# Decoder layer in float32: the scores of the windowed self-attention as one multiplication of 96 stacked rows per head

## The chip, the cores and the metric

One core of a Trainium2 chip runs the whole program. The metric is the device time of one execution in microseconds, lower is better; of several runs the median is given. TensorE multiplies, ScalarE (ACT), VectorE (DVE) and GpSimd (POOL) do the elementwise work, and SyncE (SP) issues the DMA transfers.

## What is computed

A decoder layer on x of 2 x 1024 rows of 512 numbers, in float32: windowed self-attention, cross-attention to a context of 2 x 2048 rows, and a gated feed-forward part, each behind a layer norm and added to its input. The change touches the self-attention:

```python
qkv = x @ qkv_w.T + qkv_b
q, k, v = jnp.split(qkv, 3, axis=-1)              # 16 heads of 32
q = q / (jnp.linalg.norm(q, axis=-1, keepdims=True) + 1e-6)
k = k / (jnp.linalg.norm(k, axis=-1, keepdims=True) + 1e-6)
diff = j - i
allowed = (jnp.abs(diff) <= 16) & (jnp.mod(diff, 2) == 0)
scores = jnp.where(allowed, jnp.einsum('bhnd,bhmd->bhnm', q, k), -jnp.inf)
out = jnp.einsum('bhnm,bhmd->bhnd', jax.nn.softmax(scores, axis=-1), v)
x = x + out @ out_w.T + out_b
```

Only positions of one parity see each other, so the host lays the rows out as four sequences of 512 rows, in which a row sees the 8 before and the 8 behind it.

## The kernel before

**Precision.** TensorE's fast float32 type (float32r) keeps fewer bits, so each operand is split into a rounded high part, made by ScalarE, and the rest as a low part, made by VectorE or GpSimd. A product is the sum of high x high, high x low and low x high (`three`, L187), three multiplications into one PSUM bank.

**Units.** A sequence has 16 units (`UN`): 4 groups of 4 heads, times 4 tiles of 128 keys. For a unit, `scores` (L1151) multiplies the keys of a tile with the queries in a window of 136 or 144 columns; ScalarE takes `exp` of it; GpSimd multiplies with the band (`mask`, L505); `weighted` (L1169) adds the tile's weighted values and the sums of the weights, for each head, to two PSUM banks that a group keeps for its four units. `copy_out` (L643) copies both banks, VectorE takes the reciprocal of the sums in two halves (`inverse`, L903), GpSimd multiplies (`out_scale`, L512), ScalarE rounds (`out_hi`) and GpSimd makes the low part (`out_lo`, L519). `project_out` (L1187) then multiplies all four groups of a sequence with the output weights.

**Scores before.** `heads` (L1113) turns the keys and queries of a group (four heads of 32 rows, 128 in all) by transposes. `heads_hi` (L626) and `heads_lo` (L892) write the parts. The queries are written twice, each time masked (`hmask`) to every second head, side by side, so that one multiplication of 64 rows gives two heads in 272 or 288 columns. Three products times two row halves are six multiplications for a unit.

**Slots.** The order of all queues is written by hand: a sequence is 16 slots, and slot n of sequence s holds one unit and a piece of other work. On TensorE:

- slots 0 to 3: projection of the second half of queries and keys of s
- slots 4 to 7: its values, the output projection of sequence s - 1 (one tile of 128 rows a slot, from slot 4), transposes of the input of s + 1
- slots 8 to 11: queries and keys of s + 1 (first half), transposes of sequence s - 1's result for cross-attention
- slots 12 to 15: values of s + 1, cross-attention queries of s - 1; in the last sequence the first cross-attention scores

`heads(s, 2)` is in slot 6, `heads(s, 3)` in 7, `heads(s + 1, 0)` in 14, `heads(s + 1, 1)` in 15. Slot n opens with `scores(s, n + 1)` and closes with `weighted(s, n)`; slots 7 and 15 (`LATE`) have the scores at their end. The other engines follow the same slots: GpSimd's list for n = 1 has mask 2 and `out_scale` of the last group of the sequence before, n = 2 has mask 3, its `out_lo` and two of the four bias additions (`out_bias`), then a small norm operation (`root1`), n = 3 mask 4 and the two other bias additions. `inverse` of that group is in VectorE's n = 0 and 1. SP waits for x tiles, stores and reloads the residual tile `xs` (`store`, `store_q`, L429, L442), and in the last sequence loads the first context pieces (`load_ct`).

Ring banks of PSUM (`Ring`) are taken in a fixed order (`ring_uses`); the change leaves that order as it is.

Of the kernel before, what the change touches and what calls it, by code (L numbers as in the profile page):

```python
# [49 lines left out]
LATE = (7, 15)  # L50
# [174 lines left out]
def attention_phase(nc, ctx, plan, sem, score, ident, mhalf, wait_pad, q_const, work, ring, links,  # L225
# [14 lines left out]
    qbd_h = sb("qbd_h", [P, 2, 2, SEQ], F32R)  # L240
    qbd_l = sb("qbd_l", [P, 2, 2, SEQ], F32R)
    kt_h = sb("kt_h", [P, 2, SEQ], F32R)
    kt_l = sb("kt_l", [P, 2, SEQ], F32R)
# [8 lines left out]
    over_ot = Plan(nc, plan.at)  # L252
    ot_h = sb("ot_h", [P, HG, SEQ], F32R)
# [3 lines left out]
    over_x2t = Plan(nc, plan.at)  # L257
    x2t_h = sb("x2t_h", [P, DK, SEQ], F32R)
# [10 lines left out]
    hmask = sb("hmask", [P, 2])  # L269
# [42 lines left out]
    CONSTS = 8 + HPG  # L312
# [51 lines left out]
    kq_hi = sem("kq_hi")  # L364
    s_ready = sem("s_ready")
# [13 lines left out]
    def window(i):  # L379
        lo, hi = max(0, P * i - HALO), min(SEQ, P * i + P + HALO)  # L380
        return lo, hi - lo, lo - (P * i - HALO)

    x1_v = x1_dram.rearrange("(s t p) d -> s p t d", t=ST, p=P)

    with nc.Block() as block:
        @block.sync
        def _(sp):
# [35 lines left out]
            sp.dma_start(ob_row[:], out_b.partition_broadcast(P)).then_inc(ob_landed, 16)  # L423
            for s in range(NS):
                for k in range(ST * (s + 1) + 3, min(ST * (s + 2) + 3, ST * NS)):
                    next_tile(k)
                if not s:
                    sp.wait_ge(set_lo, WO + 1)
                    sp.dma_start(xs[:], x_v[0]).then_inc(xs_landed, 16)  # L429
                if s:  # L430
                    store(s - 1)
                if s == NS - 1:
# [3 lines left out]
                    for n in range(5):  # L436
                        cross.load_ct(sp, n)
                if s:
# [19 lines left out]
        def _(pool):  # L458
            PL = nc.gpsimd

            def constants(pool):
# [4 lines left out]
                PL.memset(hmask[:], 0.0).then_inc(consts, 1)  # L466
                pool.wait_ge(consts, 5)
                for h in range(HPG):
                    PL.memset(hmask[DH * h:DH * h + DH, h % 2:h % 2 + 1], 1.0).then_inc(consts, 1)
                pool.wait_ge(consts, 5 + HPG)  # L470
# [4 lines left out]
                pool.wait_ge(consts, 7 + HPG)  # L475
# [58 lines left out]
            mask(0, 0)  # L534
            for s in range(NS):
                more = s + 1 < NS
                for n in range(UN):
                    if n not in LATE:
                        mask(s, n + 1)
                    if n == 1 and s:  # L540
                        out_scale(group(s, -1))
                    if n == 2 and s:
# [12 lines left out]
                    if n in (6, 9, 13):  # L555
                        out_scale(group(s, n // 4 - 1))
                    if n == 7:
                        mask(s, 8)
                    if n in (7, 10, 14):
                        out_lo(group(s, {7: 0, 10: 1, 14: 2}[n]))  # L560
                    if n == 15 and more:
                        mask(s + 1, 0)
# [10 lines left out]
        def _(act):  # L573
# [118 lines left out]
            heads_hi(0, 1)  # L692
            product_hi(2)
            product_hi(3)
            exp(0, 0)
            for s in range(NS):
                more = s + 1 < NS
                for n in range(UN):
                    t = n % ST
                    if t == 0 and (s or n):  # L700
                        copy_out(group(s, n // 4 - 1))
                    if n not in LATE:
                        exp(s, n + 1)
# [4 lines left out]
                    if n < 4:  # L708
                        squares(s, 1, t)
                        if n == 2 and s:  # L710
# [6 lines left out]
                    elif n < 12:  # L717
                        for m in value_parts(s, n):
# [3 lines left out]
                        if n == 10:  # L722
                            if s:
                                norm2(s - 1, 3)
# [1937 lines left out]
```

## Time and profile before

| | us |
|---|---|
| median of 3 runs | 1193.99 (1193.2 to 1194.45) |
| profiled execution, its own time | 1193.53 |
| its span in the trace | 1191.5 |
| TensorE busy | 1151.1 (97%) |
| VectorE busy | 872.4 (73%) |
| ScalarE busy | 548.3 (46%) |
| GpSimd busy | 431.7 (36%) |
| mean granted TensorE clock | 0.991 of 2.4 GHz |

Busy TensorE means that a multiplication was in flight; matmuls overlap, so a busy share near one says that the queue hardly ever waits, not that the array is full. The self-attention stage runs from about 49 to 380 us of the span, the cross-attention from there to about 830, the feed-forward part to the end.

### The profile page before, as it was taken

The numbers are of one execution on the slowest core, as the hardware profiler recorded it, in microseconds if no ns is written. First come the engines' busy times: TensorE is split into PE (matmuls) and PEld (weight loads), VectorE is DVE, ScalarE is ACT, GpSimd is POOL, SyncE is SP. The second block draws the span as 40 slices with busy tenths as digits, with TensorE's granted clock in tenths as the row PEclk, the third lists the DMA queues.
The fourth block names the chain that finished last, engine by engine and source line by source line (L and its number), as shares of the span: only waits on it lengthen the run. The fifth ranks groups of instructions, "written<-read, shape, count | busy, mean of one in ns | idle before, by whom it ended". The sixth has DMA issues, their size and how long they took to land.

```text
span 1191.5 us, 17227 instructions
## 1 busy us (share of the span) xinstructions
PE 1151.1 (97%) x6432; PEld 935.4 (79%) x6432; DVE 872.4 (73%) x1352; ACT 548.3 (46%) x862; POOL 431.7 (36%) x383
## 2 busy tenths in 40 slices
PE   7999999999989999999999997999999998999998
PEld 6777778777767888888888885878778887888886
DVE  6666675684684657876687798875899878888775
ACT  5354454455364345554445444554444445444431
POOL 1255765665753300200020034022445842444431
PEclk9899999999989999999999998999999999999999
DMA  8001010200133434333334332223311111511101
GB/s 292 9 28 45 10 63 1 80 37 23 50 111 130 166 132 142 115 101 142 121 125 149 116 121 73 80 80 123 124 54 54 54 53 63 170 53 53 53 18 71
DMA packets 53570, 103.88 MB, mean 87 GB/s; under 512 B 4848, under 2 KB 17136, under 8 KB 52464
## 3 DMA queue, kind: packets, MB, share of 16 engines
q1 hardware_dynamic: 53488, 102.78, 25.8%
q8 instruction: 52, 0.85, 0.3%
q14 instruction: 30, 0.25, 0.1%
HBM read 85.99 MB, written 16.78 MB: 86 GB/s over the span
## 4 chain that ended last, share of the span: by engine, by line
PE 81%; DVE 9%; ACT 4%; issue 3%; POOL 3%; ACTq 0%; DVEq 0%; POOLq 0%
PE work L189 15%; PE work L190 14%; PE work L191 14%; PE score L189 4%; PE score L190 4%; PE score L191 4%; PE score L2523 4%; PE score L2524 4%; PE score L2525 4%; PE score L1165 2%; PE work L2523 2%; PE work L2525 2%; PE work L2524 2%; PE score L1179 1%; PE work L1092 1%
## 5 line engine op out<-in xcount | busy, mean ns | idle before, releaser
L508 POOL TENSOR_TENSOR probs<-probs,band 128x544 f32<-128x544 f32 (+1 forms) x64 | 92.4, 1444 | 87.3 <-ACT probs L639 87.0
L2196 POOL TENSOR_TENSOR hid<-fg,hid 128x512 fp32r<-128x512 f32 x48 | 84.4, 1778 | 106.5 <-ACT hid L2263 106.5
L189 PE MATMUL score<-pt_h,cn_h 128*128 128x512 f32 x256 | 101.8, 398 | 9.5 <-DVE pt_l L1672 5.9
L1512 POOL TENSOR_TENSOR xr<-xr,bv_row 128x512 f32<-128x512 f32 x16 | 27.3, 1731 | 228.1 <-DMA xr<-x_scratch 228.1
L190 PE MATMUL score<-pt_l,cn_h 128*128 128x512 f32 x256 | 100.6, 393 | 0.0
L191 PE MATMUL score<-pt_h,cn_l 128*128 128x512 f32 x256 | 100.5, 393 | 0.0
L189 PE MATMUL work<-x_q_h,ct_h 128*128 128x512 f32 x256 | 100.3, 392 | 0.0
L191 PE MATMUL work<-x_q_h,ct_l 128*128 128x512 f32 x256 | 99.7, 389 | 0.0
L190 PE MATMUL work<-x_q_l,ct_h 128*128 128x512 f32 x256 | 99.7, 389 | 0.0
L2402 DVE SCALAR_TENSOR_TENSOR fx<-work,fx 128x512 f32<-128x512 f32 x96 | 65.7, 685 | 40.2 <-PE work L191 40.2
L189 PE MATMUL work<-wqkv_h,xt_h 128*128 128x512 f32 (+1 forms) x256 | 94.0, 367 | 0.0
L2523 PE MATMUL score<-fxt,w_hl 128*128 128x512 f32 x236 | 92.3, 391 | 1.5 <-DVE fxt L2350 0.8
L2525 PE MATMUL score<-fxt,w_hl 128*128 128x512 f32 x236 | 91.9, 389 | 0.0
L2524 PE MATMUL score<-fxt,w_hl 128*128 128x512 f32 x236 | 91.8, 389 | 0.0
L2184 POOL TENSOR_TENSOR wsum<-w_stage 128x256 f32<-128x256 f32 x24 | 18.4, 765 | 194.0 <-ACT w_stage L2220 138.3
L190 PE MATMUL work<-wqkv_l,xt_h 128*128 128x512 f32 (+1 forms) x256 | 87.5, 342 | 0.0
L191 PE MATMUL work<-wqkv_h,xt_l 128*128 128x512 f32 (+1 forms) x256 | 87.4, 342 | 0.0
L1566 ACT ACTIVATE x_pr<-x_s 128x512 f32<-128x512 f32 x52 | 33.0, 634 | 94.4 <-DVE x_s L1668 94.4
L2263 ACT CAST hid<-fg 128x512 fp32r<-128x512 f32 x48 | 29.7, 621 | 87.5 <-DVE fg L2387 52.8
L189 PE MATMUL work<-wd_h,hid 128*128 128x512 f32 x176 | 68.7, 391 | 0.6 <-DVE fx L2402 0.6
L1672 DVE TENSOR_TENSOR pt_l<-x_pr,pt_h 128x512 fp32r<-128x512 f32 x64 | 51.3, 802 | 24.4 <-ACT pt_h L1570 23.6
L191 PE MATMUL work<-wd_h,hid 128*128 128x512 f32 x176 | 68.5, 389 | 0.0
(254 smaller groups left out, 3176.1 us busy)
## 6 DMA issues: line engine op xcount, KB each, us to landing
ct_raw<-in_ctx_t SPq DMA_DIRECT2D x32, 512.0 KB, 4.6
cn_raw<-in_ctx_n SPq DMA_DIRECT2D x32, 512.0 KB, 3.8
w_stage<-in_wg_t SPq DMA_DIRECT2D x12, 512.0 KB, 4.1
w_stage<-in_wu_t SPq DMA_DIRECT2D x12, 512.0 KB, 3.8
wd_raw<-in_wd_t SPq DMA_DIRECT2D x12, 512.0 KB, 3.7
x_in<-in_x SPq DMA_DIRECT2D x16, 256.0 KB, 2.8
xs<-in_x SPq DMA_DIRECT2D x4, 1024.0 KB, 5.2
x_scratch<-xs SPq DMA_DIRECT2D x4, 1024.0 KB, 4.7
```

Of the source, the lines that this page charges most:

```text
L189: pe.matmul(out, hi_s, hi_m, start=first, stop=False)
L190: pe.matmul(out, hi_s, lo_m, start=False, stop=False)
L191: return pe.matmul(out, lo_s, hi_m, start=False, stop=last)
L508: PL.tensor_tensor(probs[:, n % 2, :, 0:w], probs[:, n % 2, :, 0:w], band[:, c0:c0 + w].unsqueeze(1).to_broadcast([P, HPG, w]), ALU.mult). ...
L1566: A.activation(pr[:, j % 2, :], s_at(j), ACT.Exp).then_inc(e_done, 1)
L1672: V.tensor_tensor(pt_l[:, j % 2, :], pr[:, j % 2, :], pt_h[:, j % 2, :].bitcast(F32), ALU.subtract)\
L2196: PL.tensor_tensor(hid[:, q, 1, :], g[:, q, :], hid[:, q, 0, :].bitcast(F32), ALU.subtract).then_inc(hidl_done, 1)
L2263: A.copy(hid[:, q, 0, :], g[:, q, :]).then_inc(hidh_done, 1)
L2402: V.scalar_tensor_tensor(xs[:, t, :], work[:, 2 + n % 2, :], WSCALE, xs[:, t, :], ALU.mult, ALU.add)\
L2523: PE.matmul(bank(key), w_h, x_h, start=first, stop=False, skip_group_check=True)
L2524: PE.matmul(bank(key), w_h, x_l, start=False, stop=False, skip_group_check=True)
L2525: last = PE.matmul(bank(key), w_l, x_h, start=False, stop=k == 1, skip_group_check=True)
```

## The change

- The four heads' keys and queries are no longer masked. `heads_hi` and `heads_lo` write four tiles (keys high and low, queries high and low) into one of three places (`turned_heads`).
- SP then moves rows by transfers from SBUF to SBUF (`stack_heads`): for each head, 96 stacked rows, keys high, low, high over queries high, high, low. A group's transfers are two halves of columns, 12 transfers in each: 4 heads x 3 parts, each 32 rows with 264 or 248 columns of keys and of queries (about 64 KB). The first half may be overwritten once unit 2 of the group before is multiplied, the second after its unit 3.
- `scores` is one multiplication of 96 rows for each head, four a unit, each of 136 or 144 columns. TensorE waits for a half (`stacked`) before units 0 and 2 of a group.
- Slot n opens with `scores(s, n)` and closes with `weighted(s, n - 1)`, without exceptions for slots 7 and 15. `copy_out`, `inverse`, `out_scale`, `out_hi`, `out_lo` and the masks move accordingly. `project_out` and `out_bias` stay in their slots.

The diff, cut to its core:

```diff
+MOVED = 3 * 4 * 16
...
+            def stack_heads(s, g, b):
+                k = group(s, g)
+                if b == 0:
+                    wait_freed(sp, ("qt", s, g))
+                if k:
+                    sp.wait_ge(s_ready, ST * (k - 1) + 3 + b)
+                c = slice(SEQ // 2 + HALO, SEQ) if b else slice(0, SEQ // 2 + HALO)
+                parts_of, (k_h, k_l, q_h, q_l) = turned_heads(g)
+                for h in range(HPG):
+                    r = slice(DH * h, DH * h + DH)
+                    for i, (of_k, of_q) in enumerate(((k_h, q_h), (k_l, q_h), (k_h, q_l))):
+                        sp.dma_start(stack[DH * i:DH * i + DH, h, :, c].bitcast(F32),
+                                     parts_of[r, of_k:of_q + 1:of_q - of_k, c].bitcast(F32)).then_inc(stacked[b], 16)
...
+            for b in range(2):
+                stack_heads(0, 0, b)
             for s in range(NS):
-                for k in range(ST * (s + 1) + 3, min(ST * (s + 2) + 3, ST * NS)):
+                for b in range(2):
+                    stack_heads(s, 1, b)
+                tiles = range(ST * (s + 1) + 3, min(ST * (s + 2) + 3, ST * NS))
+                for k in tiles[:3]:
                     next_tile(k)
                 if not s:
                     sp.wait_ge(set_lo, WO + 1)
                     sp.dma_start(xs[:], x_v[0]).then_inc(xs_landed, 16)
+                stack_heads(s, 2, 0)
+                for k in tiles[3:]:
+                    next_tile(k)
+                stack_heads(s, 2, 1)
                 if s:
                     store(s - 1)
                 if s == NS - 1:
                     wait_freed(sp, ("qk", s, 1, ST - 1))
                     cross.load_q(sp, 0)
                     wait_filled(sp, ("qt", s, 3))
-                    for n in range(5):
+                    for n in range(2):
                         cross.load_ct(sp, n)
+                stack_heads(s, 3, 0)
+                if s == NS - 1:
+                    cross.load_ct(sp, 2)
+                stack_heads(s, 3, 1)
+                if s == NS - 1:
+                    for n in range(3, 5):
+                        cross.load_ct(sp, n)
+                if s + 1 < NS:
+                    for b in range(2):
+                        stack_heads(s + 1, 0, b)
                 if s:
                     store_q(s - 1)
...
 (GpSimd)
-            mask(0, 0)
             for s in range(NS):
                 more = s + 1 < NS
                 for n in range(UN):
-                    if n not in LATE:
-                        mask(s, n + 1)
-                    if n == 1 and s:
+                    mask(s, n)
+                    if n == 2 and s:
                         out_scale(group(s, -1))
-                    if n == 2 and s:
+                    if n == 3 and s:
                         out_lo(group(s, -1))
                     if n in (2, 3) and s:
                         out_bias(s - 1, 2 * n - 4)
...
-                    if n in (6, 9, 13):
-                        out_scale(group(s, n // 4 - 1))
...
                     if n in (7, 10, 14):
-                        out_lo(group(s, {7: 0, 10: 1, 14: 2}[n]))
+                        out_scale(group(s, {7: 0, 10: 1, 14: 2}[n]))
+                    if n in (8, 11, 15):
+                        out_lo(group(s, {8: 0, 11: 1, 15: 2}[n]))
...
 (ScalarE)
             def heads_hi(s, g):
+                parts_of, (k_h, _, q_h, _) = turned_heads(g)
+                k = group(s, g)
+                if k >= 2:
+                    for b in range(2):
+                        act.wait_ge(stacked[b], MOVED * (k - 1))
                 wait_filled(act, ("kt", s, g))
-                A.copy(kt_h[:, g % 2, :], bank(("kt", s, g))).then_inc(kq_hi, 1)
+                A.copy(parts_of[:, k_h, :], bank(("kt", s, g))).then_inc(kq_hi, 1)
                 wait_filled(act, ("qt", s, g))
-                for j in range(2):
-                    A.mul(qbd_h[:, g % 2, j, :], bank(("qt", s, g)), hmask[:, j:j + 1]).then_inc(kq_hi, 1)
+                A.copy(parts_of[:, q_h, :], bank(("qt", s, g))).then_inc(kq_hi, 1)
...
-                    if t == 0 and (s or n):
+                    if t == 1 and (s or n > 1):
                         copy_out(group(s, n // 4 - 1))
-                    if n not in LATE:
-                        exp(s, n + 1)
+                    exp(s, n)
...
-                        if n == 2 and s:
+                        if n == 3 and s:
                             out_hi(group(s, -1))
...
 (VectorE)
-                for j in range(2):
-                    last = V.scalar_tensor_tensor(qbd_l[:, g % 2, j, :], bank(("qt", s, g)), hmask[:, j:j + 1],
-                                                  qbd_h[:, g % 2, j, :].bitcast(F32), ALU.mult, ALU.subtract)
-                last.then_inc(dve_freed, 1)
+                V.tensor_tensor(parts_of[:, q_l, :], bank(("qt", s, g)), parts_of[:, q_h, :].bitcast(F32),
+                                ALU.subtract).then_inc(dve_freed, 1)
...
-                    if n in (0, 1) and s:
-                        inverse(group(s, -1), n)
+                    if n in (1, 2) and s:
+                        inverse(group(s, -1), n - 1)
...
 (TensorE)
-                if i == 0:
-                    wait_freed(pe, ("qt", s, g))
+                if i % 2 == 0:
+                    pe.wait_ge(stacked[i // 2], MOVED * (group(s, g) + 1))
                 if u:
                     pe.wait_ge(exp_done, u)
-                out = [scb[:, a, 0:2 * WIN].rearrange("p (h w) -> p h w", h=2)[:, :, 0:w] for a in range(2)]
-                c = slice(P * i, P * i + P)
-                for kt, qt, first_mm, last_mm in ((kt_h, qbd_h, True, False), (kt_h, qbd_l, False, False),
-                                                  (kt_l, qbd_h, False, True)):
-                    for a in range(2):
-                        r = slice(64 * a, 64 * a + 64)
-                        last = PE.matmul(out[a], kt[r, g % 2, c], qt[r, g % 2, :, lo:lo + w],
-                                         start=first_mm, stop=last_mm)
+                for h in range(HPG):
+                    out = scb[:, h // 2, WIN * (h % 2):WIN * (h % 2) + w]
+                    last = PE.matmul(out, stack[0:3 * DH, h, 0, P * i:P * i + P], stack[0:3 * DH, h, 1, lo:lo + w],
+                                     start=True, stop=True)
...
-                    if n not in LATE:
-                        scores(s, n + 1)
+                    scores(s, n)
...
                     if n == 7:
-                        scores(s, 8)
                         heads(s, 3)
                     if n == 15 and more:
-                        scores(s + 1, 0)
                         heads(s + 1, 1)
-                    weighted(s, n)
+                    if n:
+                        weighted(s, n - 1)
+                    elif s:
+                        weighted(s - 1, UN - 1)
```

## Rows read from the trace of the kernel before

**Rows 1.** Busy time of a stretch, the third sequence: us, then each engine's busy time (count), clock, DMA

```profile
211.50:297.00 85.50, 85.00 (x708) 66.84 (x704) 56.84 (x126) 42.06 (x77) 52.30 (x49) 1.00 0.12 41
```

**Rows 2.** Timeline, TensorE, third sequence: start us, duration us, engine, line, what

```profile
219.78 0.39 PE L1165 MATMUL score<-qbd_h,kt_h 64*128 64x272 f32 x2
...
228.04 0.40 PE L1165 MATMUL score<-qbd_h,kt_h 64*128 64x288 f32 x2
...
230.18 0.40 PE L189 MATMUL work<-wo_h,ot_h 128*128 128x512 f32 x1
```

**Rows 3.** Timeline, TensorE, around one unit's weighted sums and scores

```profile
304.15 0.39 PE L190 MATMUL work<-wqkv_l,xt_h 128*128 128x512 f32 x1
304.38 0.39 PE L191 MATMUL work<-wqkv_h,xt_l 128*128 128x512 f32 x1
...
305.89 0.50 PE L189 MATMUL work<-wqkv_h,xt_h 128*128 128x512 f32 x1
306.23 0.40 PE L190 MATMUL work<-wqkv_l,xt_h 128*128 128x512 f32 x1
```

**Rows 4.** Timeline, TensorE, around weighted sums with no scores behind them

```profile
326.66 0.39 PE L191 MATMUL work<-wo_h,ot_l 128*128 128x512 f32 x1
...
327.60 0.39 PE L189 MATMUL work<-wqkv_h,xt_h 128*128 128x256 f32 x1
327.83 0.28 PE L190 MATMUL work<-wqkv_l,xt_h 128*128 128x256 f32 x1
...
328.06 0.28 PE L189 MATMUL work<-wqkv_h,xt_h 128*128 128x256 f32 x1
```

**Rows 5.** Groups of TensorE's weight loads, third sequence: busy us, mean ns

```profile
L190 PEld LDWEIGHTS work<-wqkv_l,xt_h 128*128 128x128 f32 x64 | 12.1, 189 | 1.0
```

**Rows 6.** Waits, TensorE, whole span: us in total, times, longest

```profile
PE score L1179 <- ACT o_sc L648: 1.7, 4, 0.5
```

**Rows 7.** Timeline, GpSimd, slots 2 to 4 of the third sequence

```profile
222.71 1.29 POOL L517 TENSOR_TENSOR o_sc<-o_sc,rsum 128x512 f32<-128x512 f32 x1 [4.18 <-DVE rsum L906]
223.95 1.37 POOL L508 TENSOR_TENSOR probs<-probs,band 128x544 f32<-128x544 f32 x1
225.37 1.29 POOL L522 TENSOR_TENSOR ot_l<-o_sc,ot_h 128x512 fp32r<-128x512 f32 x1
226.62 2.53 POOL L527 TENSOR_TENSOR xs<-xs,ob_row 128x512 f32<-128x512 f32 x2
229.11 0.55 POOL L483 TENSOR_TENSOR rstd<-ve,mhalf 128x1 f32<-128x1 f32 x1
...
229.98 1.36 POOL L508 TENSOR_TENSOR probs<-probs,band 128x544 f32<-128x544 f32 x1
```

**Rows 8.** Timeline, SP's issues: start, us for all of them, how many

```profile
0.79 1.33 SPq L403 DMA_DIRECT2D x_in<-in_x  x3
...
490.50 2.08 SPq L1459 DMA_DIRECT2D xr<-x_scratch  x4
```

**Rows 9.** Transfers: size of each, median us from issue to landing

```profile
x_in<-in_x SPq DMA_DIRECT2D x16, 256.0 KB, 2.8
...
out_y<-fx SPq DMA_DIRECT2D x16, 256.0 KB, 2.0
```

**Rows 10.** Timeline, VectorE's and TensorE's, first sequence: groups turned late, units behind them

```profile
87.36 0.69 DVE L895 TENSOR_TENSOR kt_l<-work,kt_h 128x512 fp32r<-128x512 f32 x1 [0.98 <-ACT kt_h L628]
...
93.83 0.40 PE L1165 MATMUL score<-qbd_h,kt_h 64*128 64x288 f32 x2
...
119.84 0.69 DVE L895 TENSOR_TENSOR kt_l<-work,kt_h 128x512 fp32r<-128x512 f32 x1
...
125.94 0.40 PE L1165 MATMUL score<-qbd_h,kt_h 64*128 64x288 f32 x2
```

**Rows 11.** Busy time of two stretches, last sequence, columns as in rows 1

```profile
344.00:350.00 6.00, 2.96 (x44) 1.72 (x36) 4.07 (x8) 4.35 (x7) 5.02 (x4) 0.95 0.00 0
350.00:356.00 6.00, 5.23 (x12) 4.11 (x13) 5.93 (x8) 2.81 (x5) 2.92 (x2) 0.50 0.00 1
```

More of the change, by code:

```diff
@@ L239, in attention_phase @@
     over = Plan(nc, plan.at)
[L240 to L243, printed above, removed]
+    stack = sb("stack", [P, HPG, 2, SEQ], F32R)
+    heads_even = sb("heads_even", [P, 4, SEQ], F32R)
     probs = sb("probs", [P, 2, HPG, WIN])
@@ L252, in attention_phase @@
     over_ot = Plan(nc, plan.at)
+    heads_ot = Plan(nc, plan.at).put("heads_ot", [P, 2 * HG, SEQ], F32R)
     ot_h = sb("ot_h", [P, HG, SEQ], F32R)
@@ L257, in attention_phase @@
     over_x2t = Plan(nc, plan.at)
+    heads_x2t = Plan(nc, plan.at).put("heads_x2t", [P, 2 * DK, SEQ], F32R)
     x2t_h = sb("x2t_h", [P, DK, SEQ], F32R)
@@ L364, in attention_phase @@
     kq_hi = sem("kq_hi")
+    stacked = [sem(f"stacked{b}") for b in range(2)]
     s_ready = sem("s_ready")
@@ L381, in window, with turned_heads @@
         return lo, hi - lo, lo - (P * i - HALO)
+    def turned_heads(g):
+        return {1: (heads_x2t, (2, 3, 4, 5)), 3: (heads_ot, (2, 3, 6, 7))}.get(g, (heads_even, (0, 1, 2, 3)))
     x1_v = x1_dram.rearrange("(s t p) d -> s p t d", t=ST, p=P)
@@ L465, in constants @@
                 PL.memset(ones[:], 1.0).then_inc(consts, 1)
[L466 to L470, printed above, removed]
+                pool.wait_ge(consts, 4)
                 PL.affine_select(out=ident[:], in_=ident[:], compare_op=ALU.not_equal, fill=1.0,
@@ L717, in _ @@
                     elif n < 12:
+                        if n == 8:
+                            out_hi(group(s, 0))
                         for m in value_parts(s, n):
@@ L721, in _ @@
                             squares(s + 1, 0, t)
-                        if n == 10:
-                            if s:
-                                norm2(s - 1, 3)
+                        if n == 10 and s:
+                            norm2(s - 1, 3)
+                        if n == 11:
                             out_hi(group(s, 1))
@@ L751, in _ @@
                     if n == 7:
-                        exp(s, 8)
                         heads_hi(s, 3)
-                        if s:
-                            wait_filled(act, ("o", s - 1, ST - 1))
-                        out_hi(group(s, 0))
                     if n == 15 and more:
-                        exp(s + 1, 0)
                         heads_hi(s + 1, 1)
@@ L1000, in _ @@
                         spread1(s + 1, {1: 0, 2: 1, 3: 2, 5: 3}[n])
-                    if n in (0, 1) and s:
-                        inverse(group(s, -1), n)
-                    if n in (5, 6):
-                        inverse(group(s, 0), n - 5)
-                    if n in (8, 9):
-                        inverse(group(s, 1), n - 8)
-                    if n in (12, 13):
-                        inverse(group(s, 2), n - 12)
+                    if n in (1, 2) and s:
+                        inverse(group(s, -1), n - 1)
+                    if n in (6, 7):
+                        inverse(group(s, 0), n - 6)
+                    if n in (9, 10):
+                        inverse(group(s, 1), n - 9)
+                    if n in (13, 14):
+                        inverse(group(s, 2), n - 13)
                     if n < 4:
@@ L1223, in _ @@
             heads(0, 0)
-            heads(0, 1)
             product(2)
             product(3)
-            pe.wait_ge(prod_lo, 2)
-            scores(0, 0)
+            heads(0, 1)
             bias_columns()
@@ L1271, in _ @@
                     if n == 7:
[L1272 removed]
                         heads(s, 3)
                     if n == 15 and more:
[L1275 removed]
                         heads(s + 1, 1)
[L1277 removed]
+                    if n:
+                        weighted(s, n - 1)
+                    elif s:
+                        weighted(s - 1, UN - 1)
             s = NS - 1
+            weighted(s, UN - 1)
             for j in (4, 5, 6):
```

22 lines of the change are left out of this document (8 added, 14 removed).

## The prediction

> **What bounds the kernel now.** I read the busy times of a stretch first, then the unit starts, then TensorE's timeline of one unit, then the queues that it waits for. In the third of the four sequences of the self-attention stage TensorE is busy for 85.0 of 85.5 us, at full granted clock [rows 1], and none of the other engines for more than two thirds. So what leaves TensorE's queue there is a gain, and what makes it wait is a loss, unless another wait goes with it. The order of its work is written by hand in slots. In the kernel before, slot n opens with the scores of unit n+1, so the score row at 219.78 opens slot 2 of that sequence, and the one at 228.04 opens slot 4: two slots of projection take 8.26 us [rows 2].
>
> **The multiplications.** Now six multiplications make a unit's scores, in three pairs of 64 rows. From the last steady matmul ahead of the weighted sums (304.38) to the second projection matmul after the scores (306.23) it is 1.85 us; two matmuls of 512 columns belong to that, 0.23 each (304.15 to 304.38), so sums and scores cost 1.39 [rows 3]. Where the sums stand alone, from 326.66 to 327.83 it is 1.17; less 0.23 for the 512-column matmul and 0.12 for the 256-column one (327.83 to 328.06 holds two) that is 0.82, with both changes of array shape in it [rows 4]. The scores therefore cost 0.57 us a unit. After the change four multiplications of 96 rows and at most 144 columns use the same shape as the projection that follows, so they need no change of shape of their own. Each needs a load of 128 columns of weights. What such a pair costs is not in this trace for 96 rows. The shortest full-height stream is the 256-column one at 0.12 [rows 4]. By columns alone it would be 144/256 of that, 0.065. Without any overlap of load and multiplication it is the 0.23 of the first matmul after a change of shape (327.60 to 327.83) [rows 4]. I take 0.12, because one load is seen for 189 ns [rows 5] and a load of the same rows cannot be put beside the last one as the 64-row pairs are; the ends stay for the range. Four cost 0.48: 0.09 saved, times 64 units is **-6 us**. At 0.065 it would be -20, at 0.23 +22.
>
> The Trainium skill ("TensorE: Matmul & The Clock Gate", Back-to-back issue gap) gives about 81 ns for a sustained pair of load and 128-column multiplication; estimated from that page, a unit would cost 0.33 us and the whole saving would be 15 us instead of 6. The same page (LDWEIGHTS) puts a load at columns over 1.2 GHz, 107 ns for 128, which agrees with my 0.12 better; no run here shows which holds for 96 rows.
>
> **ScalarE, VectorE, GpSimd.** Each group loses one masked copy on ScalarE and one masked subtraction on VectorE, and five small fills at the start go. TensorE covers this: no row has it waiting for them. They count only where they lie in the chain to the stacked rows, below. TensorE's four waits for the copied-out sums, 1.7 us in all [rows 6], stand where the copy waits for the low part; after the change the copy has a slot more behind that part. I count **-1.7**, between 0 and -1.7.
>
> **The output projection's wait.** This is the part where I expect the loss. Everything behind the weighted sums moves one slot later, but `project_out(s-1, 0)` stays in slot 4. In the third sequence GpSimd runs: normalisation of the outputs 222.71, mask 223.95, low part 225.37, two bias additions 226.62 (2.5 us), the small norm operations 229.11 to 229.98 [rows 7]. The first output matmul starts at 230.18 [rows 2], so the low part, done at 226.66, has 3.5 us to spare. After the change the normalisation waits for a reciprocal that VectorE makes one slot later: 222.71 + 4.13 = 226.84. Behind it GpSimd now has, ahead of the low part, the two bias additions, the norm operations and mask 3: 1.24 + 2.49 + 0.87 + 1.42 (start to start) [rows 7], so the low part starts at 232.86 and ends at 234.1. TensorE wants it at 230.18. Its own saving of the slots before widens the gap by 0.2: 4.1 us of waiting. ScalarE's rounding in between is ready earlier, at about five microseconds into slot 3, and is no bound. The first sequence has no such projection, the other three do; the last has neither the norm operations nor the value projection ahead, which about cancel. 3 x 4.1 = **+12.3 us**. Nothing takes this back: masks, bias and residual behind it are as late as TensorE then is.
>
> **The transfers.** 24 transfers of about 64 KB a group, 384 in all, go through SP's queue. SP needs 1.33/3 = 0.44 to 2.08/4 = 0.52 us for one issue [rows 8]; I take 0.48, so a half of 12 takes 5.8. Landing: the shortest row is 2.0 us from issue, for 256 KB [rows 9], so 1.5 beyond the end of the last issue. A half is there 7.3 us after it may start (6.8 by the shorter issue; 8.5 by the longer one and a landing of 2.8, as x_in's). TensorE waits for the first half at the start of each group. At most starts the only bound is that unit 2 of the group before has been multiplied: 0.8 us into slot 2, plus 7.3, against the 8.26 less 0.2 of two slots: just covered, in 8 of the 15 handovers. In the other 7 the heads are turned in slot 6 or 14, just before, and the chain is transposes, ScalarE, VectorE's subtraction, SP. Two of these are short, both in the first sequence. Group 2: VectorE's first subtraction starts at 87.36, the second ends 1.3 later at 88.7, the half lands at 96.0, and slot 8, now at 93.83 [rows 10], will open 0.6 earlier since unit 8's scores have left slot 7: **+2.8**. Next sequence's group 0: 119.84 + 1.3 + 7.3 = 128.4 against 125.94 - 0.6: **+3.1**. The other handovers together get **+1** as an estimate, mostly in the last sequence, where two 1 MB and two 512 KB transfers stand in front on the same queue. SP's own other work is moved past these issues: tile loads, stores and the stage's context loads start up to 12 us later; they have that much in hand except there. The first group's first half is covered by the rest of the weight product and the bias columns, which TensorE has to do ahead of slot 0; without this cover it would cost up to 7.3.
>
> **Sum.** 1193.53 (the profiled execution's own time) - 6 - 1.7 + 12.3 + 2.8 + 3.1 + 1 = **1205.0 us**; the median of the runs shown is 0.46 above that execution, so I say 1205.5.
>
> **The rivals.** *(a) The multiplications are cheap, the other side.* Place: the four score multiplications; mechanism: the next 96-row load hides behind the running multiplication and only columns count. At 0.065 a unit saves 0.31, in all 20: 1205.5 - 14 = 1191.5. It decides the sign once a multiplication costs under 0.075, where the saving passes 18 us. For: 64-row pairs run side by side today. Against: a 189 ns load for every 60 ns of columns. Chance 0.13.
> *(b) TensorE doesn't wait for the low part,* because GpSimd gets to it earlier than counted: it would need 4 us less between normalisation and low part, as much as the bias additions and mask together. 1205.5 - 12.3 = 1193. Chance 0.12.
> *(c) The clock falls after the waits.* From 344 to 350 TensorE was busy for 2.96 of 6 us, and from 350 to 356 the granted clock was 0.50, its lower level, in which twelve 512-column matmuls took 5.2 us instead of 2.8 [rows 11]. Three to five waits of 3 to 4 us could each bring 2.5 us more: 1205.5 + 3 to 12, say 1213. Against: here a thin stretch of 6 us came before, not 4. Chance 0.2.
> *(d) The transfers are slower,* since they move 32 rows in pieces of 1 KB, which no row shows. With 8.5 us a half instead of 7.3, each short handover costs 1.2 more and the covered ones turn to about 0.9 each: 2.4 + 9, less what the wait in slot 4 hides anyway: 1214. With twice the issue time SP's 24 issues no longer fit into four slots, and it is 1240 or more. Chance 0.12.
> *(e) No overlap of load and multiplication,* +28: 1233. Chance 0.04.
>
> **How the numbers follow.** My forecast, 1200 to 1210, has 0.39. About 0.2% (2.4 us) is what a measurement of this kernel can tell from no change. Faster by more: (a) with most of its chance, and the part of (b) in which the multiplications are also somewhat cheaper: 0.17. Within: the rest of (b) and of (a): 0.11. Slower: 0.72. The range leaves out the cheapest form of (a) together with (b) below, and (e) and the slow end of (d) above: 1190 to 1220.
>
> **What would show it.** Right: the first `ot_h` projection matmul of sequences 1 to 3 preceded by some 4 us of idle time ended by GpSimd's low part, and no such row before; 256 score multiplications about 0.12 apart and 0.5 a unit; waits of some 3 us for the stacked rows at units 8 and 16 of the first sequence, few elsewhere; SP issues of stack rows 0.45 to 0.52 apart. Wrong: a wait for DMA at every group's first unit (d), score multiplications 0.07 apart (a) or 0.23 apart (e), the output projection starting without a wait (b), or stretches at a granted clock of 0.5 behind the waits (c).

## The result and the profile after

The changed kernel takes 1234.71 us (median of 4 runs, 1233.64 to 1236.37) against 1193.8 for the kernel before: ratio 1.0344, interval 1.0326 to 1.0362, so 41 us slower. The forecast was 1205.5 with a range up to 1220: the direction was right, the size was not. The profiled execution's span is 1232.9 us, 41.4 above that of before.

TensorE's waits in the kernel after (us in total, times, longest):

```profile
PE score L1190 <- DMA stack<-heads_even: 17.7, 7, 5.1
PE score L1190 <- DMA stack<-heads_x2t: 15.4, 5, 5.1
PE score L1190 <- DMA stack<-heads_ot: 14.4, 5, 9.0
...
PE work L189 <- POOL ot_l L559: 2.3, 2, 1.7
...
PE work L1147 <- POOL qk L539: 1.6, 2, 1.0
```

The first three rows are the waits for stacked rows: 47.5 us. This stage's waits sum to 51.4; before they were 11.7 and the row of [rows 6] was one of them. It is gone, as forecast. The wait for GpSimd's low part, my main term, is 2.3 us instead of 12.3.

SyncE's issues after, first sequence (start, us for all, how many), the row that answers to [rows 8]:

```profile
67.46 15.70 SPq L421 DMA_DIRECT2D stack<-heads_x2t  x24
83.65 1.33 SPq L398 DMA_DIRECT2D x_in<-in_x  x3
85.03 0.42 SPq L456 DMA_DIRECT2D xs<-in_x  x1
90.65 7.99 SPq L421 DMA_DIRECT2D stack<-heads_even  x12
```

One issue costs 15.70 / 24 = 0.65 us, or 7.99 / 12 = 0.67, where I had 0.48; three loads of 256 KB between them still take 0.44 each. Landing, to compare with [rows 9]:

```profile
stack<-heads_even SPq DMA_DIRECT2D x96, 66.0 KB, 2.0
```

So a half is there 12 x 0.67 + 1.4 = 9.4 us after it may start. Slots 2 and 3 of a sequence take 4.0 us each in this trace, and the half may start only when unit 2's own scores are done, 0.5 us into slot 2: 7.6 us cover it. In slots 0 to 3 a group's 24 issues fill 16.1 of some 16.2 us; the later slots are mostly longer (4.4 to 6.8 us). In the third sequence, to which [rows 2, 3] belong (start, duration, what, idle time ahead of it):

```profile
236.50 0.39 PE L191 MATMUL work<-wqkv_h,xt_l 128*128 128x512 f32 x1
...
237.42 0.67 PE L1190 MATMUL score<-stack 96*128 96x144 f32 x4
237.92 0.45 PE L189 MATMUL work<-wqkv_h,xt_h 128*128 128x512 f32 x1
238.21 0.40 PE L190 MATMUL work<-wqkv_l,xt_h 128*128 128x512 f32 x1
...
254.68 0.69 PE L1190 MATMUL score<-stack 96*128 96x136 f32 x2 [5.09 <-DMA stack<-heads_x2t]
```

The four multiplications take 0.50 us (237.42 to 237.92), and sums and scores with two projection matmuls 236.50 to 238.21 = 1.71 against 1.85 before: 0.14 to 0.15 a unit, 9.0 to 9.6 us over 64 units. The change does what it says; the last row shows what it pays for it.

The issues alone would make a wait of 9.4 - 7.6 = 1.8 us there, not 5.09. The rest comes from SyncE's queue, whose order is fixed. Its issues in the fourth sequence, where the same place costs 4.48 us, and TensorE's two rows beside them:

```profile
331.62 0.58 SPq L406 DMA_DIRECT2D qp_scratch<-xs  x1
336.33 0.38 SPq L483 DMA_DIRECT2D xs<-in_x  x1
336.82 3.15 SPq L421 DMA_DIRECT2D stack<-heads_x2t  x5
```

```profile
333.34 0.67 PE L1190 MATMUL score<-stack 96*128 96x144 f32 x4
...
345.90 1.06 PE L1190 MATMUL score<-stack 96*128 96x136 f32 x4 [4.48 <-DMA stack<-heads_x2t]
```

Unit 2 is multiplied at 333.8, but SyncE issued the store of the residual tile at 331.6 and waits until 336.3 to issue its reload (the program has it wait for the store to land), so the rows start 3.0 us late. In the third sequence they start 2.7 us late (244.65 against 242.0). In x4 and x7 below, with four issues fewer in each half on this queue, the reload goes out ahead of unit 2 and delays nothing.

The clock behind a long wait, TensorE's timeline and then the busy time of two stretches of after, columns as in [rows 1]:

```profile
391.87 1.12 PE L1190 MATMUL score<-stack 96*128 96x136 f32 x4 [9.03 <-DMA stack<-heads_ot]
392.79 0.73 PE L189 MATMUL work<-x2t_h,wp_h 128*128 128x512 f32 x1
393.31 0.63 PE L190 MATMUL work<-x2t_l,wp_h 128*128 128x512 f32 x1
393.74 0.63 PE L191 MATMUL work<-x2t_h,wp_l 128*128 128x512 f32 x1
...
397.42 0.39 PE L191 MATMUL work<-x2t_h,wp_l 128*128 128x512 f32 x1
397.64 0.39 PE L189 MATMUL work<-x_q_h,ct_h 128*128 128x512 f32 x1
```

```profile
386.00:392.00 6.00, 0.13 (x1) 0.13 (x1) 4.88 (x6) 4.14 (x6) 3.52 (x2) 0.58 0.87 247
142.20:146.20 4.00, 4.00 (x12) 3.13 (x12) 0.00 (x0) 0.63 (x1) 1.36 (x1) 0.50 0.45 97
```

After 9 us in which TensorE had almost nothing to do (first stretch: 0.13 of 6 us), its matmuls of 512 columns start every 0.43 us for some 5 us, then every 0.23 again. That is the lower of the clock's two levels (1.2 of 2.4 GHz; 0.50 in the second stretch, behind a wait of 5.12 us that ended at 141.29). Eleven such matmuls cost 2.2 us more. Such a stretch (granted clock 0.50 to 0.59) stands behind the first group's wait and behind six others, of 2.31 to 9.03 us.

**Where 41.4 us come from:** waits 51.4 - 11.7 = +39.7, multiplications -9.8 (x1 and x2, below), and what is left is 41.4 - 39.7 + 9.8 = 11.5. The clock accounts for it: (1 - granted clock) x TensorE's busy time, summed over stretches of 0.5 us from 45 to 450, is 6.3 us before and 18.4 after, 12.1 more. The mean granted clock fell from 0.991 to 0.978.

### The profile page after: what moved, and what is told of

Its sections match the earlier page's. It is cut to its first block, busy times and chain, and to the rows that moved or that the text cites. A ratio compares the mean times of both kernels' runs of the same rounds, so it can differ in the third digit from the quotient of the medians.

```text
span 1232.9 us, 17359 instructions
## 1 busy us (share of the span) xinstructions
PE 1153.6 (94%) x6304; PEld 946.5 (77%) x6304; DVE 863.0 (70%) x1336; ACT 539.3 (44%) x846; POOL 428.9 (35%) x378
## 4 chain that ended last, share of the span: by engine, by line
PE 70%; SPq 10%; DVE 9%; DMA 3%; issue 3%; ACT 2%; POOL 2%; ACTq 0%; DVEq 0%
PE work L189 13%; PE work L190 12%; PE work L191 12%; SPq L421 10%; PE score L189 4%; PE score L191 4%; PE score L190 4%; PE score L2547 4%; PE score L2549 4%; PE score L2548 4%; PE score L1190 2%; PE work L2547 2%; PE work L2549 2%; PE work L2548 2%; PE score L1204 1%
## 5 line engine op out<-in xcount | busy, mean ns | idle before, releaser
L190 PE MATMUL work<-wqkv_l,xt_h 128*128 128x512 f32 (+1 forms) x256 | 90.3, 353 | 0.0
L191 PE MATMUL work<-wqkv_h,xt_l 128*128 128x512 f32 (+1 forms) x256 | 90.1, 352 | 0.0
L1190 PE MATMUL score<-stack 96*128 96x136 f32 (+1 forms) x256 | 45.2, 302 | 47.5 <-DMA stack<-heads_even 17.7
L2208 POOL TENSOR_TENSOR wsum<-w_stage 128x256 f32<-128x256 f32 x24 | 18.4, 769 | 194.0 <-ACT w_stage L2244 138.2
L1190 PEld LDWEIGHTS score<-stack 96*128 96x128 f32 x256 | 35.8, 202 | 62.6 <-DMA stack<-heads_x2t 16.9
```

The costliest lines, as they stand in the source:

```text
L190: pe.matmul(out, hi_s, lo_m, start=False, stop=False)
L191: return pe.matmul(out, lo_s, hi_m, start=False, stop=last)
L1190: last = PE.matmul(out, stack[0:3 * DH, h, 0, P * i:P * i + P], stack[0:3 * DH, h, 1, lo:lo + w], start=True, stop=True)
```

## The experiments

The theory: SyncE's issues, one after the other on one queue, make the rows late; the shift of the slots has its own price, the wait for GpSimd's low part, which the late rows hide. The rivals: the data movement, the multiplications, the slot order. The first four and the next four shared their runs of before (1193.49 and 1193.55); x8 and x12 have 1193.78 and 1193.86.

**x1_shift_only.** The scores of before in the slots of after: of the diff, only the moved calls.

```diff
-                    if n not in LATE:
-                        scores(s, n + 1)
+                    scores(s, n)
...
-                    if n == 1 and s:
+                    if n == 2 and s:
                         out_scale(group(s, -1))
```

> The scores of before (six multiplications, masked queries, no transfers of rows) in the slot order of after: everything behind the scores one slot later. This is the term +12.3 and the term -1.7 of the prediction by themselves. If TensorE has to wait in slot 4 of sequences 1 to 3 for GpSimd's low part as worked out, 1193.8 + 12.3 - 1.7 = 1204, with three waits of about 4 us ahead of the first output projection. If GpSimd comes to it in time (the rival), 1192 and no such waits. In the profile of after these waits are only 2.3 us in all, but there TensorE is already held up by the stacked rows in the same slot, so it does not tell.

1206.7 us, ratio 1.0110 (1.0095 to 1.0125).

```profile
PE work L189 <- POOL ot_l L522: 11.2, 3, 3.8
PE work L189 <- DVE x2t_l L825: 4.1, 3, 2.9
```

Three waits of 3.7 us on average, for which the working gave 4.1; the o_sc row is gone too. The mechanism of this term was right, and its size nearly: 11.2 us of waiting where 12.3 were forecast, +13.2 in all against +10.6. By the same sums as above, all of x1's waits are 8.8 us more than before's, and its clock costs 3.9 more: the stretches behind its three waits of 3.83, 3.83 and 3.54 us are at the lower level too (0.52 from 236.5 to 240, where before has 1.00). The second row, 3.1 us above its counterpart of before (1.0), I had not counted: the low part of the rows normalised for the next stage is late too. Where that chain lost its time was not tried.

**x2_stack_once.** Rows are stacked for the first group only; the other groups multiply what is left there.

```diff
                 k = group(s, g)
+                if k:
+                    return
```

> The kernel after, but the rows are stacked for the first group only; the other 15 groups multiply what is left there (their scores are not those of the reference; same instructions, same sizes). So the multiplications and the slot order are left and 360 of 384 transfers are gone. Theory (transfers cost the loss, multiplications gain 0.15 us a unit): 1193.8 - 9.6, plus 5 for the wait of the first group, = 1189 if nothing else waits, and about 1200 if the waits for GpSimd's low part come up now. Rival (the loss is in the shift of the slots or in the multiplications, not in the transfers): 1220 or more.

1201.67 us, ratio 1.0076 (1.0058 to 1.0094). Its waits:

```profile
PE work L189 <- POOL ot_l L561: 11.8, 3, 4.1
PE score L1193 <- issue: 4.8, 1, 4.8
```

Against after the 360 transfers are worth 33.0 us. Against x1, which has the same slots: 5.0 less, though it has the 4.8 us wait of the first group more, so the multiplications save **9.8 us**. The wait for the low part is back in full once the transfers don't hide it. So the second form of the expectation (about 1200, with those waits) held, and the rival (1220 or more) falls.

**x3_half_bytes and x4_two_parts.** The same number of transfers with half the bytes; two thirds of the transfers with all their bytes. Both leave old values in the stack, x3 in half of each half's columns, x4 in its third part (high keys, low queries).

```diff
 (x3)
+                if k:
+                    c = slice(c.start, (c.start + c.stop) // 2)
 (x4)
-                    for i, (of_k, of_q) in enumerate(((k_h, q_h), (k_l, q_h), (k_h, q_l))):
+                    for i, (of_k, of_q) in enumerate(((k_h, q_h), (k_l, q_h), (k_h, q_l))[:2 if k else 3]):
```

> The kernel after with all 384 transfers, but from the second group on each moves the first half of its columns only, 32 KB in place of 64 (the other columns keep old values). Theory (SP's 0.67 us an issue sets when the rows are there): within 5 us of after, 1230 to 1236, and the issues stay at 0.67. Rival (the moving of data, in 32-row pieces on 16 engines, sets it): the waits shrink by about half, 1215 or less; an issue time that falls with the size would point there too.

> The kernel after, but from the second group on only two of the three parts are stacked: 16 issues a group in place of 24 (the third part keeps old values). Bytes fall by a third. Theory (issue time): a half is there 4 x 0.67 = 2.7 us earlier and SP has 5.4 us a group in hand: the 15 waits for stacked rows fall from 42 us in all to about 12, the clock keeps higher, the wait for GpSimd's low part comes up in part: 1205 to 1214. Rival (landing or the chain ahead of the issues sets it): less than 10 us below after.

x3: 1232.53 us, 2 below after. x4: 1211.5, 23 below. x3's issues (duration in ns: shortest, median, longest) and then x4's waits:

```profile
L423 SPq DMA_DIRECT2D stack<-heads_even x192: 585/597/1682, 45.5 to 373.9; - x192
```

```profile
PE work L189 <- POOL ot_l L559: 11.0, 3, 4.1
PE score L1190 <- DMA stack<-heads_even: 8.5, 3, 4.1
PE score L1190 <- DMA stack<-heads_ot: 4.0, 1, 4.0
...
PE score L1190 <- DMA stack<-heads_x2t: 0.6, 1, 0.6
```

An issue takes as long for 32 KB as for 64. What counts is how many there are. In x4 the waits for rows fall from 47.5 to 13.1, that of the first group among them, and the low part's wait comes up with 11.0: so the gain is 23 us and not 34.

**x5_low_part_first and x6_once_low_part_first.** The low part made earlier, on after and on x2.

```diff
 (VectorE)
+                    if n in (1, 2) and s:
+                        inverse(group(s, -1), n - 1)
                     if n < 4:
                         qk_tile(s, 1, t)
...
 (GpSimd)
-                    if n in (2, 3) and s:
-                        out_bias(s - 1, 2 * n - 4)
-                        out_bias(s - 1, 2 * n - 3)
...
+                    if n == 3 and s:
+                        for t in range(ST):
+                            out_bias(s - 1, t)
```

> The kernel after with the low part of the outputs earlier: the reciprocals of a sequence's last group ahead of VectorE's evictions in slots 1 and 2, the rounding ahead of ScalarE's squares in slot 3, and GpSimd's four bias additions behind the low part. In the profile of x1 this wait costs 11.2 us. Theory (in after the wait for the low part is hidden behind the wait for stacked rows in the same slot, which then takes its place): 2 us below after at most, 1230 to 1235. Rival (the two add up): 11 below, 1223.

> x2 (rows stacked for the first group only, the other groups multiply what is left there) with the edit of x5. What the multiplications would give if neither transfers nor the low part held TensorE up: theory 1201.7 - 11.8 = 1190, and if more waits behind them vanish down to 1187. Rival (another wait takes the place in slot 4 or 5): 1195 or more.

x5: 1232.54 us, 2.2 below after. x6: 1187.92, 13.8 below x2, ratio to before 0.9944 (0.9924 to 0.9963). The same edit is worth 2 or 14 us, by what else ends last in slot 4. x6 has no row for ot_l among its waits. It is no version to use, since 15 groups multiply old rows, but it shows the ceiling in this slot order: with transfers for one group only, the idea gains 6 us.

**x7_two_queues.** All transfers, all bytes; the four of a half that carry high parts only are issued by ScalarE.

```diff
+            def stack_hi(k, b):
+                act.wait_ge(kq_hi, 2 * k + 2)
+                if k:
+                    act.wait_ge(s_ready, ST * (k - 1) + 3 + b)
+                move_parts(act, k // HG, k % HG, b, (0,))
```

> The kernel after, all 384 transfers with all their bytes, but the four of each half that need no VectorE (high parts of keys and queries) are issued by ScalarE and the eight others by SyncE. Theory (issues one after the other on one queue set the time): like x4, which has the same eight on SyncE: 1207 to 1216, if ScalarE, busy for 38 of 86 us in x2, can take 16 x 0.67 = 11 us more a sequence and its copies come no later. Rival (the engines that move the data, or landing): 1228 or more, since bytes and pieces are those of after.

1210.22 us, ratio 1.0144 (1.0121 to 1.0167). With the bytes and pieces of after it is 24.5 us below it, and level with x4 (1.3 below, within the spread of their runs), which has the same eight issues on SyncE. That is the strongest of the experiments: moving the data is not what made the rows late; the number of issues on one queue was.

**x9_by_dram.** A half goes to device memory in two transfers and comes back in six of 128 pieces.

```diff
+                sp.dma_start(heads_dram[k][:, 0:2, c], parts_of[:, k_h:k_l + 1, c].bitcast(F32)).then_inc(put_out, 16)
+                sp.dma_start(heads_dram[k][:, 2:4, c], parts_of[:, q_h:q_l + 1, c].bitcast(F32)).then_inc(put_out, 16)
+                sp.wait_ge(put_out, 16 * (4 * k + 2 * b + 2))
...
+                    for a, of in enumerate((of_k, of_q)):
+                        sp.dma_start(stack[DH * i:DH * i + DH, :, a, c].bitcast(F32),
+                                     heads_dram[k][:, of, c].rearrange("(h p) c -> p h c", h=HPG)).then_inc(stacked[b], 16)
```

> The kernel after, but a half's rows go to device memory in two transfers as soon as they are turned, and come back into the stack in six, each with the rows of all four heads (8 issues a half in place of 12, and only 6 of them behind the wait for unit 2; twice the bytes). Theory (issues set it): a covered handover needs 6 x 0.67 + 1.4 = 5.4 us instead of 9.4; the handovers right behind the turning (groups 2 and 0) need 8 x 0.67 + 1.4 + 2.5 for the way out = 9.3, as before. About 15 to 20 us below after: 1213 to 1220. Rival (bytes and pieces set it): at or above after, 1235 or more.

1240.17 us, 5 above after: a miss of 20. The issues did get cheap (median 432 ns); then the other parts of the chain got long.

```profile
L425 SPq DMA_DIRECT2D stack<-heads_scratch x192: 302/432/1609, 48.7 to 404.5; - x192
```

```profile
stack<-heads_scratch SPq DMA_DIRECT2D x96, 132.0 KB, 3.5
...
heads_scratch<-heads_x2t SPq DMA_DIRECT2D x8, 264.0 KB, 5.0
heads_scratch<-heads_ot SPq DMA_DIRECT2D x8, 264.0 KB, 5.7
```

I had put 2.5 us for the way out and 1.4 behind the last issue; they are 2.6 to 5.7 and 3.1 (the transfers back land 3.5 us from issue). TensorE waits in 11 places, 48.1 us in all, the longest 14.1. So the issue count is a bound only as long as landing stays at 2 us; here "fewer issues is faster" was too simple. Which part the order of SyncE's queue has in it was not tried.

**x8_two_queues_in_order and x12_query_load_early.** x7 with the edit of x5, ScalarE's transfers ahead of its squares, and the context loads of the last sequence behind the rows.

```diff
 (x8, against x7)
+                stack_heads(s, 3, 0)
                 if s == NS - 1:
                     wait_freed(sp, ("qk", s, 1, ST - 1))
                     cross.load_q(sp, 0)
...
-                stack_heads(s, 3, 0)
 (x12, against x8)
+                if s == NS - 1:
+                    wait_freed(sp, ("qk", s, 1, ST - 1))
+                    cross.load_q(sp, 0)
                 stack_heads(s, 3, 0)
                 if s == NS - 1:
-                    wait_freed(sp, ("qk", s, 1, ST - 1))
-                    cross.load_q(sp, 0)
                     wait_filled(sp, ("qt", s, 3))
```

> x7 with the edit of x5 and two changes of order: ScalarE issues its four transfers ahead of the squares of the slot, not behind them, and in the last sequence SyncE moves the first half of group 3 ahead of the loads for the next stage. x7 is at 1210.2; of its waits 7.4 us are for the low part, 2.1 for ScalarE's transfers in the third sequence, 4.8 for the half behind those loads. Theory: 1210.2 - 7.4 - 2.1 - 4.8 = 1196, and 1193 if the clock holds better; the waits of the first sequence (2.6, 2.8, and 3.0 at its start) stay. Rival (other waits take their place, ScalarE becomes late): 1203 or more.

> x8 with one load put back: in the last sequence SyncE issues the load of the next stage's first queries (x_q_raw) ahead of the first half of group 3, as in after, and only the context loads stay behind it. In x8 that load was issued 5.7 us later than in x7's place would allow, ScalarE waited 5.69 us for it with the exponentials of unit 11 behind it, and TensorE 5.5 us for those. Theory: 1202.3 - 5.5, and up to 1.7 less for the rounding behind it: 1195 to 1197. Rival (the wait for the half of group 3 comes back in its place, 4.8 us as in x7): 1201 or more.

x8: 1202.26 us, 6 above the expectation, for a reason I had made myself. ScalarE in x8:

```profile
356.49 1.04 ACT L1575 CAST x_q_h<-x_q_raw 128x1024 fp32r<-128x1024 f32 x1 [5.69 <-DMA x_q_raw<-qp_scratch]
...
357.44 0.62 ACT L682 ACTIVATE probs<-score 128x544 f32<-128x544 f32 x1
```

With the load of x_q_raw behind eight row transfers on SyncE, ScalarE stood still for 5.69 us with an exponential behind the rounding, and TensorE for 5.5. x12 puts that one load back: **1195.65 us** (12 runs), ratio to before 1.0017 (1.0005 to 1.0028), 39 us below after. Its largest waits:

```profile
PE score L1203 <- DMA stack<-heads_even: 5.3, 2, 2.9
PE work L1160 <- POOL qk L542: 4.1, 4, 1.8
```

The two waits of the first row are those of the first group and of the one whose rows are turned just before they are wanted, in slot 14 of the short first sequence. No version that moves all the rows beats the kernel before; x12 comes within 0.2% of it, and its interval still lies above 1.

**x11_shapes and x13_rows.** What makes an issue slow. Rows are stacked for the first group; then four transfers a half go where nobody reads, in four shapes (x11: both ends on the chip, one piece a row, to and from device memory; x13 below). Only the issues are read here; the times, 1204.5 and 1206.7 us, are of one run each.

```diff
 (x13)
+                    rows, pieces_n = {0: (DH, 2), 1: (2 * DH, 1), 2: (P, 1), 3: (P, 2)}[g]
+                    there = rows_dram[h][0:rows, 0:pieces_n, c]
+                    here = parts_of[0:rows, k_h:k_h + pieces_n, c].bitcast(F32)
```

> A measurement of the issue by itself. Rows are stacked for the first group only; from then on each half issues four transfers into rows that nobody reads, of four shapes: group 1 as in after (32 rows, two pieces of 1 KB, on-chip memory to on-chip memory), group 2 one piece, group 3 the same two pieces to device memory, group 0 of the next sequence from device memory. After and x3 show 0.64 to 0.67 us an issue for the first shape at 64 and 32 KB, x9 0.45 for transfers from and to device memory with more rows. If both ends on the chip are what costs: groups 1 and 2 at 0.62 or more, groups 3 and 0 at 0.50 or less. If the 32 rows or the number of pieces cost: the same for groups 1, 3 and 0, less for group 2. If neither (the issue is slow only when many follow each other): below 0.5 for all four.

> x11 with other shapes, all to device memory, four a half: group 0 of a sequence 32 rows x 2 pieces of 1 KB (64 pieces, as in after), group 1 64 rows x 1 piece (the same bytes and the same number of pieces), group 2 128 rows x 1, group 3 128 rows x 2. The issues of x11 took 0.59 us each for one or two pieces and for either direction, those of x9 with 128 pieces or more 0.40 to 0.47. If the number of rows sets it: 0.59 for group 0 alone, 0.45 for the others or falling with the rows. If the number of pieces sets it: 0.59 for groups 0 and 1, 0.45 or less for 2 and 3. If it is neither: all four alike.

Issues of x11 (32 rows: in SBUF two pieces, in SBUF one piece, to device memory, from it), then those of x13 (64 rows x 1, 128 x 1, 128 x 2, 32 x 2):

```profile
L431 SPq DMA_DIRECT2D stack<-heads_x2t x8: 585/596/597, 67.3 to 73.2; - x8
...
L431 SPq DMA_DIRECT2D stack<-heads_even x8: 512/585/996, 89.8 to 95.8; - x8
...
L431 SPq DMA_DIRECT2D rows_scratch<-heads_ot x5: 548/595/597, 105.6 to 109.6; - x5
...
L431 SPq DMA_DIRECT2D stack<-rows_scratch x8: 537/594/595, 121.1 to 127.3; - x8
```

```profile
L426 SPq DMA_DIRECT2D rows_scratch<-heads_x2t x8: 446/596/597, 66.8 to 72.5; - x8
...
L426 SPq DMA_DIRECT2D rows_scratch<-heads_even x8: 320/432/1227, 88.2 to 93.7; - x8
...
L426 SPq DMA_DIRECT2D rows_scratch<-heads_ot x8: 514/622/1371, 101.7 to 109.9; - x8
...
L426 SPq DMA_DIRECT2D rows_scratch<-heads_even x8: 549/595/597, 120.2 to 126.1; - x8
```

Neither the two ends, the direction nor the bytes set it: 32 x 1, 32 x 2 and 64 x 1 pieces all take 0.59 us, and only 128 x 1 takes less, 0.43. The theory of x11 (both ends on the chip) falls. Of x13's, neither the rows nor the pieces alone fit: 128 x 2 takes 0.62. And even the shape doesn't fix it, for x9 sends out 128 rows x 2 pieces of the same tiles, two transfers at a time and not four, in 0.40 to 0.47:

```profile
L418 SPq DMA_DIRECT2D heads_scratch<-heads_x2t x8: 432/435/1169, 58.6 to 347.2; - x8
```

What sets the time of an issue stays open. The argument needs only that the stack's own shape takes 0.65 us from issue to issue, which after and x3 show.

## Why the prediction was wrong in size and right in sign

- **The multiplications: right.** 0.12 us each, 0.48 a unit forecast; 0.50 measured, and -9.8 us in all where I had -6: the steady unit cost 0.15 less, not 0.09. Rivals (a) and (e) fall. The rule of the Trainium skill weighed there ("TensorE: Matmul & The Clock Gate", Back-to-back issue gap), 81 ns for a pair of load and 128-column multiplication, is not what 96 rows of fp32r do here: 125 ns a pair at full clock.
- **The output projection's wait: right by itself, hidden in the sum.** +12.3 forecast; 11.2 and 11.8 in x1 and x2, 11.0 in x4; 2.3 in after, because a wait for rows opens slot 4 (5.09 us in the third sequence) and GpSimd is done when it ends. I had seen this for (d) alone ("less what the wait in slot 4 hides anyway"); the forecast counted those handovers as covered. Rival (b) has the outcome of after, for a wrong reason.
- **The transfers: the step that failed.** "SP needs 0.44 to 0.52 us for one issue" came from loads of 256 KB; the stack's issues take 0.65 to 0.67. The landing, 1.4 behind the last issue, was right (I had 1.5). But 12 x 0.18 = 2.2 us more took a half from 7.3 to 9.4 us, past the 7.6 to 8.5 that cover it where unit 2 is the bound, so 12 of the 15 handovers wait for more than 0.3 us, and not two. The two that were named came out as 4.56 and 5.12 us where 2.8 and 3.1 were forecast. And 24 issues of 0.67 fill slots 0 to 3 there, so SyncE's store and reload make the next half 2.7 and 3.0 us later still (5.09 and 4.48). I worked out (d) with a half at 8.5 us (1214) and with the issue time doubled (1240 or more), and gave it 0.12: reality lies between them. The uncertainty of this one number deserved more: by the prediction's own working a half landed 0.8 + 7.3 = 8.1 us into two slots of 8.06, with nothing to spare at eight handovers.
- **One cover in the last sequence: a second step that failed.** "The other handovers together get +1" left out how short slots 10 and 11 of the last sequence are. The longest wait, 9.03 us, is there: unit 2 is multiplied at 379.6, and TensorE wants the next group's rows at 391.87 - 9.03 = 382.84, 3.2 us later. Even a half of 7.3 us would cost 4 there. With eight issues a half, in x4, the wait there is still 3.96 us. In x12, which moves that half ahead of the context loads, 0.20 is left; 2.4 us of other waits (for ScalarE's normalised rows) end in the slots before it and hide part of it.
- **The first group's cover: wrong.** I had "covered by the rest of the weight product and the bias columns": 5.1 us in after, 4.8 in x2. I had given up to 7.3 without this cover, and put nothing in the sum.
- **The clock, rival (c): right as a mechanism,** 11.5 us by the ledger above (12.1 by the granted clock) where it had 3 to 12. Its counter-argument, that a wait of 4 us might be too short, falls: x1's waits of 3.5 to 3.8 us bring the lower level too.

In one line, against the kernel before: shift of the slots +13.2 (x1), first group +4.8, multiplications -9.8, transfers of the other groups +33.0 (x2 to after, in which they also hide 9.5 us of the shift's wait), in all 41.2.

## What to carry to other kernels

Before rows are moved by many small transfers, take the time of one issue of that very shape, multiply by their number on one queue, and compare with the time of the step they must fit into: here the transfers cost 33 us where 7 were forecast, and taking four of twelve issues off the queue gave 24.5 back. Look for the shortest such step in the whole schedule, not only for the usual one. Spread issues over a second engine's queue, with each placed where its own inputs are ready, and leave the loads that another engine waits for in front. Waits that end in the same slot don't add: mending one (x5, 2 us) shows its worth only when the other is gone (x6, 14 us).

## What the runs showed that was not expected

- An issue's time does not follow bytes: 0.60 us for 32 KB and for 64 KB, to and from device memory as well and on ScalarE's queue too (0.59 to 0.62); 0.43 for 128 rows of one piece, 0.33 to 0.38 for a 1 MB store in the kernel before.
- With issues on two queues, four of ScalarE's took 2.5 to 3.0 us in most places of x12 and 3.3 to 4.14 in four (the longest at 84.26); what held those up was not seen.
- The clock was low behind waits of 5 us in the middle of dense work, and behind the one of 9.03 us, during which the DMA engines were busy for 0.87 of a 6 us stretch, VectorE for 4.88 us of it and ScalarE for 4.14: other engines' work did not keep TensorE's clock up there.
